# Three late experts in place of two, and the end stage reordered around them (attention layer and mixture of experts in one kernel, 1 core)

## What is computed

```python
x = layernorm(x + attention(x))               # 4096 tokens of 256
# mixture of experts, E = 8: each expert picks its k = 4096/8 = 512 tokens
G_t, idx_t = top_k(softmax(xf @ Wr + br).T, k)
mid = silu(tokens @ W_up[group] + b_up)       # 512 x 682, two experts share one W_up
out = mid @ W_down + b_down                   # 512 x 256
y = zeros.at[idx].add(G * out)                # a token may be picked by several experts
x = layernorm(x + y)                          # over every token's 256 values
```

## Time and profile before

| | |
|---|---|
| time, three runs | 437.48, 437.6, 438.69 us (median 437.6) |
| the profiled execution | 435.77 us |
| its span, first to last instruction | 434.0 us |
| mean granted TensorE clock | 0.925 |
| busy: PE, DVE, POOL, ACT | 366.4, 235.1, 165.4, 147.7 us |
| the chain that ended last, share of the span | PE 62%, DVE 12%, POOL 11%, DMA 4%, ACT 1% |
| TensorE's last matmuls (L816, expert 7) begin | 403.74 us |
| one up tile's silu on ScalarE (L1360, mean) | 0.687 us |
| POOL's last issue (L1521) begins | 426.48 us |

### The profile page before, as it was taken

How to read it: one execution, slowest core, us unless ns; L and a number is a source line. 1 busy time by engine, 2 the same in 40 slices (tenths; PEclk the granted TensorE clock), 3 DMA queues, 4 the chain that set the end, 5 groups by cost and what they waited for, 6 DMA issues and landing times.

```text
span 434.0 us, 5612 instructions
## 1 busy us (share of the span) xinstructions
PE 366.4 (84%) x1639; PEld 241.8 (56%) x1639; DVE 235.1 (54%) x885; ACT 147.7 (34%) x350; POOL 165.4 (38%) x250
## 2 busy tenths in 40 slices
PE   5999999899997980114899999999999999999930
PEld 4788886567775650003438566474756657464620
DVE  2555553787888888878663736513130311059450
ACT  1433332444685885330031120403112030347600
POOL 0310043001567884001703542436344243564853
PEclk9999999999999995555699999999999999999985
DMA  8945544500132554900301452515433272689641
GB/s 270 302 137 171 168 145 147 178 0 2 49 123 100 194 170 148 11 0 2 87 12 52 88 116 63 76 51 109 120 84 48 53 138 69 113 280 373 219 163 48
DMA packets 49630, 50.75 MB, mean 117 GB/s; under 512 B 12137, under 2 KB 42562, under 8 KB 49602
## 3 DMA queue, kind: packets, MB, share of 16 engines
q1 hardware_dynamic: 43650, 40.32, 31.6%
q0 software_dynamic: 5952, 10.10, 11.6%
HBM read 32.97 MB, written 17.43 MB: 116 GB/s over the span
## 4 chain that ended last, share of the span: by engine, by line
PE 62%; DVE 12%; POOL 11%; issue 6%; DMA 4%; ACT 1%; POOLq 0%; SPq 0%; DVEq 0%; ACTq 0%
PE ps L816 16%; PE ps L785 15%; PE ps L615 7%; PE ps L623 6%; PE ps L599 6%; PE ps L757 3%; PE ps L693 3%; POOL rstd L1412 3%; DVE qexp L1031 2%; PE ps L706 2%; PE ps L772 1%; DMA out<-h_all 1%; DMA heads<-ysum,idx 1%; POOL ysum L1465 1%; POOL xg L1458 1%
## 5 line engine op out<-in xcount | busy, mean ns | idle before, releaser
L816 PE MATMUL ps<-wdn_s,ht_all 128*128 128x256 f32 (+1 forms) x384 | 95.4, 394 | 0.0
L785 PE MATMUL ps<-xgt,wup_s 128*128 128x512 f32 (+1 forms) x192 | 88.0, 610 | 0.1
L816 PEld LDWEIGHTS ps<-wdn_s,ht_all 128*128 128x128 f32 (+1 forms) x384 | 67.7, 189 | 25.0 <-issue 18.4
L1360 ACT ACTIVATE ht_all<-ps,bup_s 128x512 f32<-128x512 f32 (+1 forms) x48 | 33.0, 687 | 122.6 <-PE ps L785 122.6
L1458 POOL DMA_INDIRECT xg<-table,idx x32 | 32.4, 1013 | 89.8 <-DVE idx L1158 46.4
L785 PEld LDWEIGHTS ps<-xgt,wup_s 128*128 128x128 f32 (+1 forms) x192 | 33.3, 182 | 48.0 <-issue 48.0
L1465 POOL DMA_INDIRECT ysum<-yb,idx x24 | 40.6, 1693 | 46.5 <-DVE yb L1190 41.0
L1190 DVE TENSOR_SCALAR yb<-ps,gate 128x256 f32<-128x256 f32 x24 | 11.6, 484 | 55.7 <-PE ps L816 55.7
L599 PE MATMUL ps<-wqkv_s,heads 128*128 128x264 f32 x128 | 33.8, 413 | 5.9 <-DMA heads<-xt 5.2
L706 PE MATMUL ps<-wp_s,turned 128*128 128x264 f32 x128 | 33.7, 385 | 0.0
L599 PEld LDWEIGHTS ps<-wqkv_s,heads 128*128 128x128 f32 x128 | 26.1, 205 | 11.0 <-issue 6.2
(11 more groups left out here) (191 smaller groups left out, 526.4 us busy)
## 6 DMA issues: line engine op xcount, KB each, us to landing
wdn_s<-wdn SPq DMA_DIRECT2D x8, 640.0 KB
heads<-xt SPq DMA_DIRECT2D x8, 512.0 KB, 3.8
h_all<-x SPq DMA_DIRECT2D x8, 512.0 KB, 5.1
ht_all<-xtq SPq DMA_DIRECT2D x8, 512.0 KB, 3.6
table<-x SPq DMA_DIRECT2D x32, 128.0 KB, 1.7
ysum<-x SPq DMA_DIRECT2D x32, 128.0 KB, 1.8
h_all<-ysum SPq DMA_DIRECT2D x8, 512.0 KB, 8.7
out<-h_all SPq DMA_DIRECT2D x8, 512.0 KB, 5.2
```

The lines of the kernel that those rows point to most:

```text
L785: mm = pe.matmul(ps[0:width, f % 2, :], wup_s[:, c, f * P:f * P + width], xgt[:, c, :], start=(c == 0), stop=(c == C - 1))
L816: mm = pe.matmul(ps[:, bank, 0:D], mid[0:rows_, f, j * P:(j + 1) * P], wdn_s[0:rows_, f, :], start=(f == 0), stop=(f == FT - 1))
L1360: act.activation(mid[0:width, f, :], ps[0:width, f % 2, :], ACT.Silu, bias=bup_s[0:width, e // GS, f:f + 1]).then_inc(s_mid, 1)
```

## The change

Three experts are late: `LATE` becomes 5, and experts 5, 6 and 7 go through gathered rows, sums and writes; expert 5 no longer adds in the transfer. In detail:

- `yb` holds expert 5's sums, two further pieces of `early` those of experts 6 and 7, and three pieces their normed rows.
- SP loads blocks 0 to 3, then `wup` of the last group (experts 6 and 7), then blocks 4 to 7. It stores all 8 blocks before it loads expert 7's `wdn`.
- TensorE waits for all four of expert 5's sums before it turns expert 7's tokens; each down group of experts 6 and 7 waits for the sum that last used its bank.
- VectorE makes expert 5's four sums with one block's moments after each, then the other blocks, then the sums of 6 and of 7; expert 7's rows are normed in pairs.
- ScalarE norms four rows ahead of expert 6's six up tiles, two after each of the first five (ten), and everything else of its rows before expert 7's up tiles.
- POOL: each write of a sum waits for that sum (`into`), and there are two rounds of writing and gathering.

```diff
-LATE = E - GS
-NORMS = NT + GS * KT
+LATES = 3
+LATE = E - LATES
+NORMS = NT + LATES * KT
...
-            for e in range(1, E - 1):
+            for e in range(1, LATE + 1):
...
-            for b in range(2):
-                sp.wait_ge(s_fin, TB * (b + 1))
-                store_block(b)
-            sp.wait_ge(s_dmm, KT * (E - 1))
-            load_down(E - 1)
-            for b in range(2, NB - 2):
+            sp.wait_ge(s_ybfree, LATE + 2)
+            for b in range(NB // 2):
+                load_rows(b)
+            sp.wait_ge(s_umm, FT * (LATE + 1))
+            load_up((LATE + 1) // GS)
+            for b in range(NB // 2, NB):
+                load_rows(b)
+            sp.wait_ge(s_dmm, KT * (LATE + 1))
+            load_down(LATE + 1)
+            for b in range(NB - 2):
...
+            sp.wait_ge(s_dmm, KT * (E - 1))
+            load_down(E - 1)
...
+                if e == LATE + 1:
+
+                    pe.wait_ge(s_y, KT * (LATE + 1) + 2)
                 if not last:
                     turn(e + 1)
...
-                    if last:
-
-                        pe.wait_ge(s_y, LATE * KT + (j + 3))
+                    if e > LATE:
+
+                        pe.wait_ge(s_y, (e - 1) * KT + (j + 3))
+                        if not last and j >= 2:
+                            pe.wait_ge(s_xt, C * (e + 2))
...
             for j in range(KT):
                 late_sum(LATE, j, yb)
-                if j % 2 == 0:
-                    block_moments(3 + j // 2)
-            for b in range(5, NB):
+                block_moments(j)
+            for b in range(KT, NB):
                 block_moments(b)
...
+            gates(E - 1)
             dve.wait_ge(s_ylate, 2 * 16 * KT)
+            for j in range(KT):
+                late_sum(LATE + 1, j, y_sixth)
+            dve.wait_ge(s_y, KT * (LATE + 2) + 2)
+            moments(NT + KT, lambda t: y_sixth[:, t, :], KT)
+            for j in range(KT):
+                centred(NT + KT + j, o_late[1][:, j, :], y_sixth[:, j, :], s_fin_sixth)
...
             expert(LATE)
-            for tile in range(3 * TB):
+            for tile in range(TB):
                 normed_row(tile)
 
+            for f in range(FT - 1):
+                up(LATE + 1, f)
+                for tile in range(TB + 2 * f, TB + 2 * f + 2):
+                    normed_row(tile)
+            up(LATE + 1, FT - 1)
+            turn(E - 1)
+            for tile in range(TB + 2 * (FT - 1), NT - 2 * TB):
+                normed_row(tile)
+            for j in range(KT):
+                normed(NT + j, o_late[0][:, j, :], yb[:, j, :])
             for f in range(FT):
                 up(E - 1, f)
-                normed_row(3 * TB + f)
...
+            def into(e, y):
+
+                for j in range(KT):
+                    pool.wait_ge(s_y, KT * e + (j + 3))
+                    pool.indirect_dma_start(out=ysum[:, :], out_offset=bass.IndirectOffsetOnAxis(ap=idx[:, e, j:j + 1], axis=0),
+                                            in_=y[:, j, :], in_offset=None).then_inc(s_into, 16)
...
             late_rows(0)
+            gather(E - 1)
...
-            pool.wait_ge(s_y, KT * (LATE + 1) + 2)
...
+            into(LATE, yb)
             factors(4 * TB, 2 * TB)
+            pool.wait_ge(s_into, 16 * KT)
+            late_rows(1)
             factors(6 * TB, 2 * TB, False)
             factors(NT, KT)
-            pool.wait_ge(s_into, 16 * KT)
-            late_rows(1)
-
+
+            into(LATE + 1, y_sixth)
             pool.wait_ge(s_out, 16 * NB)
             for j in range(KT):
...
+                late_out(LATE, j, s_fin)
+            factors(NT + KT, KT, False)
+            pool.wait_ge(s_into, 2 * 16 * KT)
+            late_rows(2)
             pool.wait_ge(s_late, 16 * KT)
             for j in range(KT):
...
+                late_out(LATE + 1, j, s_fin_sixth)
+            for pair in range(KT // 2):
+                factors(NT + 2 * KT + 2 * pair, 2, False)
+                if pair == 0:
+                    pool.wait_ge(s_late, 2 * 16 * KT)
+                for j in (2 * pair, 2 * pair + 1):
+                    late_out(E - 1, j, s_fin_seventh)
```

More of the change, by code:

```diff
@@ L262, in build @@
         y_late = early[:, 0:KT * D].rearrange("p (j d) -> p j d", j=KT)
-        y_last = early[:, 6 * KT * D:7 * KT * D].rearrange("p (j d) -> p j d", j=KT)
-        o_late = early[:, KT * D:3 * KT * D].rearrange("p (k j d) -> p k j d", k=GS, j=KT)
+        y_sixth, y_last = (early[:, at * KT * D:(at + 1) * KT * D].rearrange("p (j d) -> p j d", j=KT) for at in (5, 6))
+        o_late = [early[:, at * KT * D:(at + 1) * KT * D].rearrange("p (j d) -> p j d", j=KT) for at in (1, 2, 4)]
         stats = early[:, 3 * KT * D:4 * KT * D]
@@ L386, in build @@
         s_fin_last = sem("s_fin_last")
+        s_fin_sixth = sem("s_fin_sixth")
         s_fin_seventh = sem("s_fin_seventh")
@@ L560, in _, with load_rows @@
                 load_down(e)
-            sp.wait_ge(s_ybfree, LATE + 2)
-            for b in range(NB):
+            def load_rows(b):
                 tiles = slice(b * TB, (b + 1) * TB)
@@ L1249, in centred_block @@
                     centred(tile, h_all[:, tile, 0:D], h_all[:, tile, 0:D], s_fin_last)
-            for b in range(3):
-                block_moments(b)
+            spread(E - 1)
+            numbers(E - 1)
+            gates(LATE + 1)
             dve.wait_ge(s_add, 16 * KT * LATE)
@@ L1270, in _ @@
                 dve.wait_ge(s_y, KT * (E - 1) + 2 + 2 * pair + 2)
-                moments(NT + KT + 2 * pair, lambda t: y_last[:, 2 * pair + t, :], 2)
-            for j in range(KT):
-                centred(NT + KT + j, o_late[:, 1, j, :], y_last[:, j, :], s_fin_seventh)
+                moments(NT + 2 * KT + 2 * pair, lambda t: y_last[:, 2 * pair + t, :], 2)
+                for j in (2 * pair, 2 * pair + 1):
+                    centred(NT + 2 * KT + j, o_late[2][:, j, :], y_last[:, j, :], s_fin_seventh)
         @block.scalar
@@ L1381, in _ @@
             expert(LATE)
-            for tile in range(3 * TB):
+            for tile in range(TB):
                 normed_row(tile)
+            for f in range(FT - 1):
[8 more added lines that the diff above has]
+                normed(NT + j, o_late[0][:, j, :], yb[:, j, :])
             for f in range(FT):
                 up(E - 1, f)
-                normed_row(3 * TB + f)
-            for tile in range(3 * TB + FT, NT - 2 * TB):
-                normed_row(tile)
-            for j in range(KT):
-                normed(NT + j, o_late[:, 0, j, :], yb[:, j, :])
         @block.gpsimd
@@ L1491, in late_rows, with late_out @@
                                             in_offset=bass.IndirectOffsetOnAxis(ap=idx[:, LATE + k, j:j + 1], axis=0)).then_inc(s_ylate, 16)
+            def into(e, y):
[3 more added lines that the diff above has]
+                                            in_=y[:, j, :], in_offset=None).then_inc(s_into, 16)
+            def late_out(e, j, done):
+                pool.wait_ge(done, j + 1 if e > LATE else NT - 2 * TB + j + 1)
+                pool.indirect_dma_start(out=out[:, :], out_offset=bass.IndirectOffsetOnAxis(ap=idx[:, e, j:j + 1], axis=0),
+                                        in_=o_late[e - LATE][:, j, :], in_offset=None).then_inc(s_late, 16)
             pool.wait_ge(s_ybfree, LATE + 2)
             late_rows(0)
+            gather(E - 1)
             for b in range(4):
```

17 lines of the change are left out of this document (3 added, 14 removed).

## The result

The median of 11 runs is **435.2 us** (434.74 to 437.07), against 437.6 for 11 runs of the kernel before: a ratio of 0.9952 [0.9931, 0.9973], 2.1 us faster by the ratio. The forecast was 436.0 and faster; the time is inside its range.

The account below looks back on a forecast made before the run. Bound: a chain from the last additions' landing through POOL, VectorE, loads, ScalarE and stores, beside TensorE. It starts 24.8 us earlier, 23.2 go into added work, so 437.6 - 1.6 = 436.0 us; range 433.2 to 439.6.

Parts of the forecast that it names:

- The start: Chain begins at expert 4's last adding issue, 351.49 instead of 376.29: 24.80 us earlier; first sum at 366.11.
- Step 3: POOL's first write: 0.48 us to first issue, 3.87 to the last, then block factors 2.04; through at 384.3.
- it does nothing: Rival: omitted links of 0.1 to 0.2 us add up to 1.6, giving 437.6; chance 0.28 shared with TensorE as bound.
- Step 4: Expert 6's gather waits for the first writes to land, 3.2 us, plus 0.8 to issue; starts at 385.3.
- Steps 5 to 8: From expert 6's gather through second write (395.8), third gather (407.3) and scatters to the last issue at 424.9.
- the waits are shorter: Rival: writes land in 2.4 us and three wake-ups take 0.3 instead of 0.8, 2.0 us more gain, 434.0; chance 0.15.
- step 8: Last scatter waits for expert 6's, 2.96 us behind its last issue, so 419.3; last issue 424.9.
- The stores: Last block stores, issued near 394.9, land by 400.1, so the wait for all blocks (415.48 before) leaves the chain.
- Held transfers: Slower rival: block transfers hold up indexed gathers and writes, 3.9 us in all, giving 439.9; chance 0.17.
- TensorE's cover: TensorE's end at 415.74 could move to 418.85 before the last expert's second pair waits: 3.1 us.
- The end: From the last issue to the end of the span, 7.52 us, taken as fixed.
- The sign: Forecast is wrong in step 4 or 5 if POOL or VectorE stands idle there over 1 us.

Follow-up runs that it names:

- pool_plus: Changed kernel plus one dead eight-column power (1.67 us) on POOL between the second write and expert 5's scatter; ratio to the kernel before 1.0015.
- fewer_waits: Changed kernel without POOL's four waits for block loads 0 to 3 ahead of the first write; ratio to the kernel before 0.9943.
- pairs_together: Changed kernel with expert 7's rows normed in one set of four instead of in pairs; ratio to the kernel before 0.9933.
- sums_first: Changed kernel with VectorE making expert 6's sums before block 7's normed tiles instead of after; ratio to the kernel before 0.9953.
- pe_plus: Changed kernel plus four dead matmuls on TensorE ahead of expert 7's up tiles; ratio to the kernel before 0.9959.
- wup_last: Changed kernel with the last wup load behind all eight block loads instead of four; ratio to the kernel before 1.0027.
- own_waits_alone: Kernel before, with only each write of expert 6's sums waiting for its own sum; ratio to the kernel before 1.0004.

## Why the prediction was right

In relative times, forecast from 351.49 and measured from 353.06:

| place (POOL's first issue) | forecast | measured |
|---|---|---|
| first gather of `ysum` rows | 4.67 | 4.61 |
| first sum (VectorE) | 14.62 | 14.51 |
| first write | 26.0 | 26.50 |
| expert 6's gather | 33.8 | 33.88 |
| second write | 44.3 | 43.88 |
| third gather | 55.8 | 55.03 |
| first of the last four scatters | 67.8 | 67.02 |
| last issue | 73.4 | 72.14 |

**The start** was right to 0.1 us: the chain begins 24.8 us earlier, with gathers that meet the same loads as before. **That nearly all of it is given back** was right as well, in the right places: of 24.8 the stage keeps 2.85, the forecast said 1.6. The third write, gather and scatter, POOL's powers and the rounds of VectorE between take the rest, and pool_plus shows that they stand in the row that sets the end.

**Step 3** took 0.48 before the first write; it is 1.14. Nine waits stand there; four of them cost 0.47 (fewer_waits), and 0.75 pass between the last semaphore instruction and the issue. That is the sort of link that the rival "it does nothing" counted.

**Step 4** took 3.2 for the writes' landing and 0.8 behind it. These four landed in 2.4 to 4.1, median 3.2, but POOL was busy with the factors until 386.46 and its gap is the plain 0.48: the landing was no wait, and POOL's lateness of step 3 cancelled against the 0.8. The 2.3 us of the Trainium skill ("DMA: Bandwidth & Descriptors", section "Anatomy of one DMA — SWDGE (gpsimd) path") for the landing itself held for the quickest of these writes (2.4), not for their median (3.2). The second four took 3.6 to 5.5 with the DMA share at 0.89. The 3.2 set between two rows was the better measure of the landing, but the path did not need it. (The share of 1.06 beside the writes of before is that of 382 to 404; over 397 to 406, while they were under way, it was 0.84.)

**Steps 5 to 8** went by the forecast, with three gaps smaller: the second write 0.3 behind the end of its first sum (396.17 + 0.48 to 396.94) in place of 0.8, the third gather 0.18 in place of 0.48, the last pair's first issue about 0.3 behind its normed tile in place of 0.8. These are the 0.4, 0.3 and 0.5 us by which the measured column runs ahead. The 0.8 came from the write before, which I read as the price of a wake-up. It is the price of one kind only: there the wait stands in a semaphore instruction of its own, and an indexed issue follows such an instruction by 0.74 to 0.78 wherever POOL stands still for it in this stage. At the second write and at the last pair the wait is part of the issue itself, which then follows what it waits for by 0.3, as at the stores before (0.27). This is the term that was mis-sized, and the rival "the waits are shorter", with 434.0, was nearer to the truth in its mechanism: the time fell between it and the forecast. The 2.96 of step 8 came out (417.11 to 420.08), but it is not the landing that it was taken for: the normed tile and 0.74 behind it set it (pairs_together).

**The stores** are off the chain, as forecast: the last is issued at 396.2 and all have landed by 396.2 + 3.6 = 399.8, 2.3 us ahead of the scatter. sums_first uses this up. **Held transfers**, the slower rival, did not come: the first sum is 0.1 early, and expert 6's gather landed 2.9 to 4.3 behind its issues, under the 5.3 that the normed tiles hide. **TensorE's cover** was given as 3.1 us; pe_plus shows 3.0 and wup_last 3.15. **`wup`** landed at 359.00 + 10.0 = 369.0, that is 367.4 on the forecast's clock, within its 366 to 369 (the midpoint in that sum is 358.2, not 358.5, which changes nothing); wup_last shows what it would have cost otherwise. **The ten rows** cost nothing and, not forecast either way, gain nothing. **The pairs** I counted at their price without asking what the four together would cost: a microsecond less. **The end** of the span behind the last issue, taken as fixed at 7.52, is 8.1 with three late experts and 7.5 again in own_waits_alone: POOL's drain is 0.6 longer. So the stage was 1.3 shorter than forecast and the end 0.6 longer; that the time came so near to the forecast is in part the luck of these two. **The sign** for steps 4 and 5, POOL or VectorE idle for more than 1 us, was no sign: by the forecast's own times, too, VectorE waits over 6 us for the power of blocks 6 and 7 (measured 6.82) and POOL over 2 for the second write's sum (1.97).

## What to carry to other kernels

Where a stage is a chain through one engine's serial issues, starting it earlier by N buys only N less what must be added to the chain; count the issues (here twelve more, at 1.26 us each 15 us of the 22 that were given back), then the work of the other engines between them, and ask for each gap which of its waits ended last. A gap read once is not a price for another place: the 0.83 us at the write before stood behind a semaphore instruction of its own, and where the issue itself carries the wait it was 0.3. And compare two profiles of a late stage from its own first instruction, since the code ahead of it can vary by more than the change is worth.

## What was not expected of the hardware

- An indexed issue of POOL follows a semaphore instruction that stands ahead of it by 0.74 to 0.78 us in this stage (397.25, 422.58 before; 357.67, 379.56, 420.08 in the change), and 0.27 to 0.30 the event itself where the issue carries the wait (415.75 before; 396.94, 423.87 in the change).
- Waits that are already met still cost POOL time: 1.13 to 1.14 us ahead of the first write with nine of them, 0.67 with five.
- The same code ahead of the end stage brought it to its start at 351.49 in one profile, at 355.54 in another (own_waits_alone) and at 356.33 in a third (wup_last): 5 us, twice what the change gained. Much of it goes with TensorE's clock: over the first 100 us it was granted 1.00 in the five profiles with a start of 351.49 to 353.49, 0.98 in the five at 354.18 to 355.14, and 0.97 in the two last.
- A weight load of 682 KB lands in 4.0 us alone (the last one in the kernel before), 10.0 behind four block loads and 11.2 behind eight.
- A wait of 4.92 us of TensorE's brought it to half its clock for some 4 us behind it, in wup_last.
